# Cross-attention and FFN on one core: the LayerNorm statistics ahead of the second exponential, and a new order of VectorE's middle steps

## The reference

```python
def block(x, ctx, fside):
    # x: (16, 1024, 512), ctx: (16, 64, 512), fside: (16, 16)
    xl = layernorm(x)                                  # no weights
    xn = layernorm(ctx, ln1_w, ln1_b)
    ln = layernorm(xl, ln2_w, ln2_b)
    q = heads(ln @ Wq) * (1 + fside) + fside           # per batch and head
    k, v = split(xn @ Wkv)
    p = softmax(q @ k.T / 8)                           # over 64 context rows, per head
    x = x + merge(p @ v) @ Wout
    return x + tanh(layernorm(x) @ W @ A1 @ A2 + bias)
```

## Time and profile before

| | |
|---|---|
| median of 3 runs | 2192.18 us (2190.67 to 2192.84) |
| the profiled execution | 2190.67 us, span 2188.7 us |
| PE busy | 2110.7 us (96%) |
| DVE busy | 1651.7 us (75%) |
| ACT busy | 1326.2 us (61%) |
| POOL busy | 1347.4 us (62%) |
| granted TensorE clock | 0.995 |

### The profile page before, as it was taken

The page is one execution under the profiler, slowest core; times in us unless marked ns, Lnnn a source line. Parts: engine busy times, 40 slices in busy tenths (PEclk is TensorE's granted clock), DMA queues, the critical chain, the costliest instruction groups (busy, mean ns, idle before and its releaser), DMA issues.

```text
span 2188.7 us, 35272 instructions
## 1 busy us (share of the span) xinstructions
PE 2110.7 (96%) x9664; PEld 1745.2 (80%) x9664; DVE 1651.7 (75%) x2747; ACT 1326.2 (61%) x3159; POOL 1347.4 (62%) x1492
## 2 busy tenths in 40 slices
PE   6998999999999999999999999999999999999997
PEld 5877888787888878788888878888887888888786
DVE  6746777777777777777778777777777777777875
ACT  3354666666666666666666666666666665666654
POOL 4426757576665757576575757666575766657564
PEclk9999999999999999999999999999999999999999
DMA  6435546364554535355453545445363545546353
GB/s 209 154 102 154 163 138 183 113 181 140 159 158 142 177 124 182 125 164 158 145 173 123 181 130 167 145 153 175 123 183 119 182 140 161 160 128 183 120 174 120
DMA packets 376812, 334.33 MB, mean 153 GB/s; under 512 B 71248, under 2 KB 268112, under 8 KB 376784
## 3 DMA queue, kind: packets, MB, share of 16 engines
q1 hardware_dynamic: 376784, 333.99, 49.3%
HBM read 191.23 MB, written 142.61 MB: 153 GB/s over the span
## 4 chain that ended last, share of the span: by engine, by line
PE 79%; DVE 6%; ACT 6%; issue 4%; POOL 4%; DMA 1%; SPq 0%; ACTq 0%; DVEq 0%; POOLq 0%
PE bank L153 33%; PE bank L826 17%; PE bank L158 16%; PE bank L833 9%; PE bank L616 3%; POOL area L1000 3%; DVE bd L559 1%; DVE row_max L907 1%; DVE area L902 1%; ACT bank L693 1%; ACT bd L576 1%; ACT pT_hi L851 1%; ACT area L686 1%; PE bank L617 1%; ACT M_hi L635 1%
## 5 line engine op out<-in xcount | busy, mean ns | idle before, releaser
L1000 POOL TENSOR_TENSOR area<-area,row_max 128x256 f32<-128x256 f32 x512 | 360.7, 726 | 504.8 <-DVE row_max L907 504.8
L846 ACT ACTIVATE area<-area 128x512 f32<-128x512 f32 x256 | 161.9, 632 | 468.5 <-POOL area L1000 468.4
L1007 POOL TENSOR_TENSOR area<-area,row_inv 128x512 f32<-128x512 f32 x256 | 319.6, 1267 | 172.5 <-DVE row_inv L916 172.5
L826 PE MATMUL bank<-N_hi,pT_hi 128*128 128x512 f32 x1024 | 403.3, 394 | 4.5 <-ACT pT_hi L851 4.4
L153 PE MATMUL bank<-M_hi,xT_hi 128*128 128x512 f32 x1024 | 399.2, 390 | 0.0
L153 PE MATMUL bank<-M_lo,xT_hi 128*128 128x512 f32 x1024 | 399.1, 390 | 0.0
L826 PE MATMUL bank<-N_lo,pT_hi 128*128 128x512 f32 x1024 | 399.0, 390 | 0.0
L902 DVE SCALAR_TENSOR_TENSOR area<-bank,rs,area 128x512 f32<-128x512 f32 x256 | 191.4, 748 | 203.3 <-PE bank L158 202.1
L158 PE MATMUL bank<-M_hi,xT_lo 128*128 128x512 f32 x1024 | 274.7, 390 | 5.9 <-POOL xT_lo L720 5.9
L833 PE MATMUL bank<-N_hi,pT_lo 128*128 128x512 f32 x1024 | 276.2, 391 | 0.0
L933 DVE TENSOR_TENSOR pT_lo<-turned,pT_hi 128x512 fp32r<-128x512 f32 x256 | 225.0, 879 | 48.0 <-ACT pT_hi L851 48.0
(11 more groups left out here) (130 smaller groups left out, 4188.1 us busy)
## 6 DMA issues: line engine op xcount, KB each, us to landing
p_scratch<-area SPq DMA_DIRECT2D x256, 256.0 KB, 2.0
p_moved<-p_scratch SPq DMA_DIRECT2D x1024, 64.0 KB, 2.0
area<-x_dram SPq DMA_DIRECT2D x128, 256.0 KB, 3.2
area<-x_turned_dram SPq DMA_DIRECT2D x128, 256.0 KB, 3.7
x_scratch<-area SPq DMA_DIRECT2D x128, 256.0 KB, 3.3
x_moved<-x_scratch SPq DMA_DIRECT2D x512, 64.0 KB, 2.0
y_dram<-area SPq DMA_DIRECT2D x128, 256.0 KB, 2.2
kv_scratch<-area SPq DMA_DIRECT2D x32, 256.0 KB, 2.3
```

What stands on the lines that cost most here:

```text
L826: pe.matmul(O_ps[:], pT_hi[:, k * P:(k + 1) * P], n_cols(mv, k), start=(k == 0 and mv is N_hi), stop=False)
L846: act.activation(s, s, ACT.Exp).then_inc(s_ex[q], 1)
L1000: last = pool.tensor_tensor(s, s, row.to_broadcast([P, 2, 4, J2]), ALU.subtract)
L1007: pool.tensor_tensor(s, s, inv, ALU.mult).then_inc(s_p[q], 1)
```

## The change

On ScalarE, `ln1_stats` moves from behind `pT_hi_part(1)` to a place right behind `xT_split_hi`, ahead of `exp(1)`. On VectorE, `turn_p(1)` moves behind `inverse_sums(0)` and the first two `m_dve` parts, the FFN bias step moves up to follow it, and `inverse_sums(1)`, `m_dve` parts 2 and 3 and `pT_lo_part(1)` come after that. No instruction is added or taken away.

```diff
             if has["following"]:
                 xT_split_hi(act, t + 1, (m + 1) % 2)
+                ln1_stats(act, t + 1, (m + 1) % RING)
             if first:
                 fold_hi(act, t, range(6), s_n, s_nh, N_fold[2])
             if has["scores"]:
...
             if has["attn"]:
                 pT_hi_part(1)
-            if has["following"]:
-                ln1_stats(act, t + 1, (m + 1) % RING)
             if has["fold_n"] and not first:
                 v_prepare_act(act, t // 8)
...
             if has["attn"]:
                 pT_lo_part(0)
-                turn_p(1)
             if has["scores"]:
                 inverse_sums(0)
             if has["fold_m"]:
                 m_dve(dve, t + 1, range(2))
-            if has["scores"]:
-                inverse_sums(1)
             if has["attn"]:
-                pT_lo_part(1)
-            if has["fold_m"]:
-                m_dve(dve, t + 1, range(2, 4))
+                turn_p(1)
             if ended(t, m):
                 dve.wait_ge(s_f, t - 2)
                 at_least(dve, s_y, t - 3)
                 dve.wait_ge(s_rs2, t - 2)
                 dve.scalar_tensor_tensor(out=hid, in0=F_ps[:], scalar=rs2[:, 0:1], in1=ffn_bias_row[:],
                                          op0=ALU.mult, op1=ALU.add).then_inc(s_fb, 1)
+            if has["scores"]:
+                inverse_sums(1)
+            if has["fold_m"]:
+                m_dve(dve, t + 1, range(2, 4))
+            if has["attn"]:
+                pT_lo_part(1)
             if has["fold_m"]:
                 m_dve(dve, t + 1, range(4, 6))
```

## The result

| | before | after |
|---|---|---|
| median of 4 runs | 2191.93 us (2190.67 to 2192.84) | 2228.90 us (2228.15 to 2229.72) |
| the profiled execution | 2190.67 us, span 2188.7 us | 2224.78 us, span 2222.8 us |

The change makes the kernel slower: ratio 1.0169, 95% interval 1.0151 to 1.0186. That is 37 us by the medians and 34.1 us by the two profiled executions; the forecast was 2222 us, 2203 to 2236.

The account below looks back on a forecast made before the run. TensorE, busy 96% of the span, was taken to bound the kernel. Terms 12.4 + 5.9 + 9.2 + 2.3 + 0 = 29.8 us brought the profiled 2190.67 us to 2220.5, given as a 2222 us median, range 2203 to 2236.

Parts of the forecast that it names:

- The bound and the room: Middle slots: TensorE has no hole, 0.72 us of room; stalls about 0.20 us each, 62 x 0.20 = +12.4 us.
- The row of the second pass: TensorE's second matmul started 0.39 us after the second half of `pT_hi` ended; the first half's row gave 0.45.
- The rival in which all of them fit: Moved statistics fit ScalarE's idle stretch, TensorE never waits for `pT_hi`: 2179 us, faster; chance 0.08.
- m == 4: Slot where GpSimd first prepares the keys: a stall of 0.38 us, 15 x 0.38 + 0.20 = +5.9 us.
- m == 5: Slot with a late exponential: 0.6 us taken, 15 x 0.6 + 0.2 = +9.2 us (5.5 to 12.2).
- m == 0: Batch change: earlier `bd` casts, but `diag_lo` meets GpSimd's reads; +0.15 us per change, 15 x 0.15 = +2.3 us.
- the rival of an unhindered pair: m == 0: the `diag_lo` pair keeps its turn or meets nothing: 2206 us; chance 0.20.
- m == 7 and VectorE: Later VectorE work eats 1.65 of 1.80 us idle time in m == 7: taken as 0, bounds -0.3 and +0.9.
- only change places: Middle slots: VectorE's FFN step, turn, sums and `pT_lo` are covered if the second `pT_lo` is ready in time.
- The late bias copy: m == 7: bias copy 0.9 us later, absorbed by TensorE's hole; if not, 13.5 more, 2235 us, chance 0.11.
- The sum: Whole kernel: 12.4 + 5.9 + 9.2 + 2.3 + 0 = 29.8 us slower; median 2222 us, chance 0.57.
- The signs: Changed profile: middle slots 13.8 us, `L826` waiting for `pT_hi` some 90 times, last statistic about 3.4 us behind first exponential.

Follow-up runs that it names:

- Half of the statistics: The whole change, but only sum and mean ahead of the second exponential, square and variance behind `pT_hi`: 2195.7 us, ratio 1.0021.
- the run without that meeting: The whole change, with GpSimd's `ku_lo` made one slot later, in m == 5 ahead of the first `normalise`: 2209.9 us, ratio 1.0088.
- the two runs on m == 0: Kernel before with `v_prepare_act` ahead of the statistics in m == 0: 2187.5 us; the same plus GpSimd's power ahead of `xT_lo` there: 2171.4 us.
- VectorE's half: Kernel before with only the VectorE part of the change, statistics at their old place: 2219.1 us, ratio 1.0129.
- the two kernels with the late turn and late statistics: Kernel before with only the change's VectorE part, 2219.1 us, and kernel before with only its later second turn, 2223.7 us.
- FFN step's kernel: Kernel before with only the FFN bias step moved ahead of the second sums: 2205.1 us, ratio 1.0062.

## Why the prediction was right, and where it was off

- **The bound and the room: right.** TensorE has no hole in a middle slot, and 0.72 us of room before the second attention pass. The row of the second pass, 0.39 us, was the right one of the two: the changed kernel shows 0.40, the slots 13.80, the term 12.4 us. (The working's "remaining 0.91" is not 2.04 less 1.03, which is 1.01, but the delay by its own starts, 4.13 less 3.23.) Half of the statistics, which fit, cost nothing. The rival in which all of them fit is out.
- **m == 4: right.** 0.39 us against 0.38.
- **m == 5: right mechanism, size wrong.** The term "15 x 0.6 + 0.2 = +9.2 us" measured 16.9 us, 1.11 us a slot. The working had the bare cost at 0.84 and then let 0.1 to 0.45 come back through an altered meeting of `diag_lo` and `xT_lo`; its own upper value, 0.7, makes 10.7 us and not the 12.2 of its bound. Nothing came back. With the key preparation at its old time the slot is 0.86 longer than before, which is the bare cost; with it early, `diag_lo` takes 2.48 us, VectorE's line is later, and another 0.25 is added. The cause of the late exponential is `x2T_lo` behind `ku_lo`, shown by the run without that meeting.
- **m == 0: right.** +0.12 us in the mean against +0.15. Timeline of the changed kernel's `diag_lo` pair and of `xT_lo`:

```profile
1059.44 2.98 DVE L559 TENSOR_TENSOR bd<-area,bd 64x512 fp32r<-64x512 f32 x2
...
1060.15 1.72 POOL L720 TENSOR_TENSOR xT_lo<-area,xT_hi 128x512 fp32r<-128x512 f32 x1
```

  1.89 us in the earlier trace rows became 2.98, and the pair ends 0.55 us behind `xT_lo`, as the working had it: the earlier casts were eaten by the clash, so the rival of an unhindered pair is out. The rule of the Trainium skill (SBUF — State Buffer, "Who interferes with whom") that the two engines exclude each other agrees with this row, and with the 2.56 us against 1.57 of the two runs on m == 0.
- **m == 7 and VectorE: right in the number, by luck in part.** I took 0, with -0.3 as the lower bound; it was -0.31. Behind it stand -1.0 from the earlier ScalarE work and +0.7 from VectorE's new order, and the working, which set 1.65 us of later work on VectorE against 1.80 us of its idle time, had neither of them in its size. That VectorE's steps "only change places" holds for middle slots (13.60 with VectorE's half alone) and failed elsewhere: alone, that half costs 30.2 us by its profiled execution, 10.3 in m == 7 by the longer slot and 11 more by the fallen clock, 3.8 in m == 5, 2.4 in m == 0 and 2.7 behind the last batch's slots. The working looked only at the whole change. There the early statistics keep TensorE's wait for an M part at 0.8 us or less, and the clock stays up. The late bias copy was absorbed, as said (TensorE waits for it 2.2 us in all, and m == 7 is shorter than before); that rival is out.
- **The sum.** It was 29.8 us; 34.1 by the profiled executions. m == 5 is 7.7 too small, m == 7 4.7 too large, and the 1.6 us of the ramps were left out. Between the profiled execution and the median lie 4.1 us after and 1.3 before; no run tells from what.
- **The signs.** The last statistic starts 3.40 us behind the first exponential, as forecast (3.4). "A wait of `L826` for `pT_hi` some 90 times" is there 111 times, in the weight loads; the matmuls show 19.

## What to carry to other kernels

Where one engine is never idle, measure for each of its waits how much room its last input has, and hold every moved instruction against that room: here 1.0 us ahead of the exponential was free, and 2.04 us cost 0.20 in each slot that had no hole. Move work only in the slots that have a hole: the same early statistics made m == 7 a microsecond shorter and, confined to it, the kernel 15 us faster. Making an input ready early gains little while its consumer collides with another engine's read: the early input alone won 3 us, and moving that read aside 16 more. And take a change apart before you trust its sum: here the two halves cost 19 us more than the whole, and 11 of these 19 are slots in which the granted clock fell, which it did with one half alone and not with both.

## What was not expected of the hardware

- The granted clock fell within slots with m == 7 in the two kernels with the late turn and late statistics, in nine and ten of the 15: 26.00 us at a mean of 0.93 against 24.75 us at 1.00 for the same work in VectorE's half. The clock there is 1.2 instead of 2.4 GHz for a part of the slot, from 0.5 to 2.0 us after TensorE had paused 1.7 to 1.8 us for M part 6. But the pause does not always bring it down. In VectorE's half the first of these rows is from a slot of 24.75 us, where it did not fall, the second from one of 26.00:

```profile
1163.14 0.38 PE L616 MATMUL bank<-bd,Wq_hi 128*128 128x256 f32 x1 [1.80 <-ACT area L634]
...
1290.80 0.38 PE L616 MATMUL bank<-bd,Wq_hi 128*128 128x256 f32 x1 [1.74 <-ACT area L634]
```

  In the FFN step's kernel it fell once in a slot with m == 0, after a pause of 1.74 us for `bd`, and the slot took 22.74 us instead of 21.1; the other m == 0 slots have the same pause and kept the clock. In the kernel before, where TensorE's waits in full slots are 1.4 us at most, and in the whole change, 1.2 at most, it did not fall in a full slot. What decides it beyond the pause, no run shows. A hole that grows by 0.7 us thus cost up to 1.9.
- Two short VectorE subtractions in a row do not keep GpSimd out: in the changed kernel's m == 0 the second starts at 1060.75, 0.01 us after the first ended, and still ends 0.55 us behind the `xT_lo` that GpSimd had begun at 1060.15. The pair would take 1.38 us by the 0.69 us of the earlier trace rows, and took 2.48 to 2.98 beside `normalise` and `xT_lo`.
